# Later places for evictions, norms, shares and loads in a period of sixteen steps, and a later bias addition

## The reference

```python
xn = (x - mean) / sqrt(var + 1e-5)
q, k, v = split_heads(xn @ Wq.T), split_heads(xn @ Wk.T), split_heads(xn @ Wv.T)
diff_sq = max(|q|^2 + |k|^2 - 2 q.k, 0)
cosh_arg = 1 + 2 * diff_sq / max((1 - |q|^2) * (1 - |k|^2), 1e-6)
attn = softmax(-arccosh(cosh_arg))
out = (attn @ v) @ Wo.T
w = int4_rounded(kernel)
ffn = xn @ w + bias + (xn @ a) @ b
```

## Time and profile before

| | us |
|---|---|
| median of 3 runs | 2607.86 (2605.85 to 2612.83) |
| profiled execution, time | 2615.11 |
| its span | 2613.4 |
| TensorE busy | 2318.2 (89%) |
| ScalarE busy | 2159.3 (83%) |
| VectorE busy | 2086.7 (80%) |
| GpSimd busy | 252.1 (10%) |

### The profile page before, as it was taken

The page is one execution under the profiler, slowest core; times in us unless marked ns, Lnnn a source line. Parts: engine busy times, 40 slices in busy tenths (PEclk is TensorE's granted clock), DMA queues, the critical chain, the costliest instruction groups (busy, mean ns, idle before and its releaser), DMA issues. The chain is left out here.

```text
span 2613.4 us, 44986 instructions
## 1 busy us (share of the span) xinstructions
PE 2318.2 (89%) x17416; PEld 810.0 (31%) x17416; DVE 2086.7 (80%) x2780; ACT 2159.3 (83%) x2022; POOL 252.1 (10%) x75
## 2 busy tenths in 40 slices
PE   4889989999999999999999999999999999977774
PEld 1433333333333333333333333333333333321111
DVE  7778878888887888887888888888888887866663
ACT  2258898889888888988898888888889888999990
POOL 1011011101101110110111011011101101000000
PEclk8999999999999999999999999999999999999997
DMA  3542332444244343534524433443435344243314
GB/s 124 147 133 70 78 101 81 122 120 126 88 120 133 93 110 112 144 93 118 133 82 121 127 113 106 122 133 93 110 113 135 100 113 125 81 129 84 84 39 118
DMA packets 357001, 285.82 MB, mean 109 GB/s; under 512 B 81296, under 2 KB 296464, under 8 KB 356784
## 3 DMA queue, kind: packets, MB, share of 16 engines
q1 hardware_dynamic: 356784, 282.91, 39.3%
HBM read 160.30 MB, written 121.63 MB: 108 GB/s over the span
## 5 line engine op out<-in xcount | busy, mean ns | idle before, releaser
L416 ACT ACTIVATE root<-pU 128x1024 f32<-128x1024 f32 x1024 | 1016.0, 1027 | 31.5 <-PE pU L189 31.1
L420 ACT ACTIVATE root<-root 128x2048 f32<-128x2048 f32 x512 | 981.0, 1916 | 58.1 <-DVE root L653 56.2
L189 PE MATMUL pU<-QS,KS 100*128 100x512 f16 x2048 | 623.0, 387 | 175.9 <-ACT root L416 172.7
L653 DVE TENSOR_SCALAR root<-root 128x2048 f32<-128x2048 f32 x512 | 627.7, 1226 | 82.1 <-ACT root L416 78.8
L658 DVE TENSOR_TENSOR root<-root 128x2048 f32<-128x2048 f32 x256 | 584.5, 2283 | 14.9 <-ACT root L420 13.7
L199 PE MATMUL pO<-root,VX 128*32 128x512 f32 x4096 | 556.0, 613 | 2.3 <-ACT root L420 2.3
L767 POOL TENSOR_TENSOR xt<-xt,bias_b 128x512 f32<-128x512 f32 x64 | 243.3, 3803 | 1908.3 <-DVE xn L552 1901.6
L189 PEld LDWEIGHTS pU<-QS,KS 100*128 100x128 f16 x2048 | 139.6, 98 | 727.8 <-ACT root L416 387.3
L213 PE MATMUL pZ<-root,ones 128*32 128x512 f32 x2048 | 276.7, 611 | 1.0 <-DVE root L658 1.0
L565 DVE TENSOR_REDUCE nrm<-sqr 128x16 f32<-128x512 f32 x128 | 87.5, 683 | 144.7 <-ACT sqr L445 144.7
L257 PE MATMUL pM<-Wvh,xT 128*128 128x512 f16 x512 | 181.5, 399 | 2.6 <-ACT qk L441 2.6
(11 more groups left out here) (106 smaller groups left out, 2253.2 us busy)
## 6 DMA issues: line engine op xcount, KB each, us to landing
v_d<-v_o SPq DMA_DIRECT2D x64, 264.0 KB, 2.1
k_d<-kx SPq DMA_DIRECT2D x64, 264.0 KB, 2.1
KT<-k_d SPq DMA_DIRECT2D x64, 264.0 KB
VX<-v_d SPq DMA_DIRECT2D x64, 264.0 KB
xt<-in_x SPq DMA_DIRECT2D x32, 512.0 KB, 4.6
res_d<-f_o SPq DMA_DIRECT2D x64, 256.0 KB, 2.1
QS<-qh_d SPq DMA_DIRECT2D x128, 128.0 KB
KS<-kh_d SPq DMA_DIRECT2D x128, 128.0 KB
```

The costliest lines, as they stand in the source:

```text
L189: mm = pe.matmul(pU[:, col:col + HALF], KS[i][:, h, j * P:(j + 1) * P], QS[i][:, h, half * HALF:(half + 1) * HALF], start=True, stop=True)
L416: act.activation(root[:, q % RING, cols], pU[:, cols], ACT.Square).then_inc(squared, 1)
L420: act.activation(root[:, q % RING, :], root[:, q % RING, :], ACT.Sqrt).then_inc(rooted, 1)
L653: v.tensor_scalar(root[:, q % RING, :], root[:, q % RING, :], CS * CS, CS * CS, ALU.max, ALU.subtract).then_inc(clamped, 1)
```

## The change

Nothing is computed otherwise. In each engine's `behind` and in ScalarE's loop the step at which a piece stands is another:

- TensorE: f's projection of even periods at steps 12 and 13 (was 13 and 14).
- ScalarE: pO's copy after the square of step 5 (was before that of step 4), pZ's after step 8 (was before step 6), v's eviction at 8 (was 7), the variance's root at step 0 of the next even period (was 14 of the odd one).
- VectorE: norms at 4 and 6 (were 3 and 5), `normalise` at 7 (6), `aug_rows` at 9 (8), `inverse` at 2 (0), `divide` at 1 (4), `take_f` at 14 in even periods and at 0 of the next period for odd ones (15).
- GpSimd: the bias addition of a tile also waits until q of that tile is transposed, two periods later than before.
- SP: stores of attention, k and extra rows one step later, the first half of a stack's load behind KV's copies (step 13, was 9), the other half in step 3 of the odd period, f's store and x's load with the later `take_f`.

```diff
--- before.py
+++ after.py
@@ -329,12 +329,10 @@
                         elif n + 1 < NT:
                             pe.wait_ge(x_split, n + 2)
                         transpose_feat(n, 0, 0 if even else 1)
-                    if even and k == 13:
+                    if k == 12:
                         pe.wait_ge(feat_split[0], n + 1)
-                    if not even and k == 12:
-                        pe.wait_ge(feat_split[0], n + 1)
-                    if even and k in (13, 14):
-                        project(n, "f", 0, 6 * k - 78, 6 * k - 72)
+                    if even and k in (12, 13):
+                        project(n, "f", 0, 6 * k - 72, 6 * k - 66)
                     elif not even and k in (12, 13, 14):
                         project(n, "f", 1, 4 * k - 48, 4 * k - 44)
                     if even and k == 14:
@@ -457,10 +455,10 @@
                         take_qk(n, 0, 0)
                     elif k == 4:
                         take_qk(n, 1, 1)
-                    elif k == 7:
+                    elif k == 8:
                         take_v(n, 1)
-                if k == 14 and p % 2 and n + 3 < NT:
-                    deviation((n + 3) // 2)
+                if k == 0 and p % 2 == 0 and p and n + 2 < NT:
+                    deviation((n + 2) // 2)
 
             deviation(0)
             deviation(1)
@@ -476,16 +474,16 @@
                 take_v(n, 1 - n % 2)
                 if n % 2:
                     deviation((n + 3) // 2)
-            for s in range(16 * PERIODS + 8):
+            for s in range(16 * PERIODS + 9):
                 p, k = s // 16, s % 16
-                if k == 4 and p:
-                    take_v_sums(p - 1)
-                if k == 6 and p:
-                    take_one_sums(p - 1)
                 if s < 2 * QUADS:
                     square(s)
+                if k == 5 and p:
+                    take_v_sums(p - 1)
                 if s % 2 and 0 <= (s - 3) // 2 < QUADS:
                     sinh((s - 3) // 2)
+                if k == 8 and p:
+                    take_one_sums(p - 1)
                 if p < PERIODS:
                     behind(p, k)
 
@@ -660,25 +658,26 @@
             def behind(p, k):
                 n, o, even = p + LEAD, p - LEAD, p % 2 == 0
                 if n < NT:
-                    if k == 0 and even and n + 2 < NT:
+                    if k == 2 and even and n + 2 < NT:
                         inverse((n + 2) // 2)
-                    if k == 3:
+                    if k == 4:
                         norm(n, 0)
                     if k == 5 and n + 1 < NT:
                         split_x(n + 1, 0)
-                    if k == 5:
+                    if k == 6:
                         norm(n, 1)
                         factors(n)
-                    if k == 6:
                         scale_qk(n)
-                        if n + 2 < NT:
-                            normalise(n + 2)
-                    if k == 8:
+                    if k == 7 and n + 2 < NT:
+                        normalise(n + 2)
+                    if k == 9:
                         aug_rows(n)
                 if k == 0 and p % 2 and n - 1 < NT:
                     split_feat(n - 1, 1, 1)
+                if k == 0 and even and p and n - 1 < NT:
+                    take_f(n - 1, 1)
                 if o >= 0:
-                    if even and k == 4:
+                    if even and k == 1:
                         divide(o)
                     if k == (9 if even else 10):
                         take_o(o, 0)
@@ -694,8 +693,8 @@
                 if n < NT:
                     if k == 14 and not even and n + 3 < NT:
                         moments((n + 3) // 2)
-                    if k == 15:
-                        take_f(n, 0 if even else 1)
+                    if k == 14 and even:
+                        take_f(n, 0)
 
             dve.up(v.memset(ones[:, :], V_SCALE))
             dve.up(v.memset(flag[:, :], 0.0))
@@ -764,6 +763,8 @@
             def add_bias(n):
                 t = xt[n // 2 % 3][:, n % 2, :]
                 g.wait_ge(xn_done, n + 1)
+                if n >= LEAD:
+                    g.wait_ge(featT_made[0], n + 1)
                 g.tensor_tensor(t, t, bias_b[:, :], ALU.add).then_inc(xb_done, 1)
 
             def everywhere(dst, col, after):
@@ -906,21 +907,13 @@
                     load_res(o)
                 if k == 8 and n < NT:
                     store_v(n)
-                if k == 8 and p:
+                if k == 9 and p:
                     store_att(p - 1)
                 if k == 9 and last_of_block:
                     load_z((o + 1) // TPB, p)
-                if k == 9 and n < NT:
+                if k == 10 and n < NT:
                     store_k(n)
                     store_aug(n)
-                if k == 9 and even and 2 <= p and p // 2 + 1 < PERIODS // 2:
-
-                    sy.wait_ge(summed_up, p * JC)
-                    if (p // 2 + 1) % KC == 0:
-                        all_stored(n)
-                    load_stack(p // 2 + 1, 0)
-                    if (p // 2 + 1) % KC:
-                        load_stack(p // 2 + 1, 1)
                 if k == (10 if even else 11) and o >= 0:
                     store_out(o)
                 if k == 12 and not even and o >= 0 and not last_of_block and o + 1 < NT:
@@ -932,11 +925,21 @@
                     store_feat(n)
                 if k == 12 and even:
                     pass_kv(p)
-                if k == 15 and n < NT:
+                if k == 13 and even and 2 <= p and p // 2 + 1 < PERIODS // 2:
+
+                    sy.wait_ge(summed_up, p * JC)
+                    if (p // 2 + 1) % KC == 0:
+                        all_stored(n)
+                    load_stack(p // 2 + 1, 0)
+                if k == 3 and not even and 3 <= p and p // 2 + 1 < PERIODS // 2 and (p // 2 + 1) % KC:
+                    load_stack(p // 2 + 1, 1)
+                if k == 15 and even and n < NT:
                     store_f(n)
-                    if not even and n + 5 < NT:
-                        sy.wait_ge(var_done, (n + 3) // 2)
-                        load_x((n + 5) // 2)
+                if k == 1 and even and p and n - 1 < NT:
+                    store_f(n - 1)
+                    if n + 4 < NT:
+                        sy.wait_ge(var_done, (n + 2) // 2)
+                        load_x((n + 4) // 2)
 
             load_x(0)
             sy.dma_start(idn[:, :], io["ident"]).then_inc(small_loaded, 16)
```

## The result

The changed kernel takes 2471.64 us (2470.7 to 2475.46, 4 runs) against 2608.57 us: a ratio of 0.9476, interval 0.946 to 0.9493. That is 137 us less, where 118 were forecast (2490, range 2450 to 2560).

What follows compares the result with a forecast made beforehand. TensorE and ScalarE in lockstep bound the kernel; 108 us from the main stretch, 14 from the first, 3 from the last, less 8 for divisors, gave 117 off the profiled 2615.1; less 7.3 for the median: 2490 us, range 2450 to 2560.

Steps and rivals of the forecast that it cites:

- What bounds the kernel: Main stretch: TensorE and ScalarE run in lockstep, TensorE the busier; its waits, 88.6 us for squares and 34.6 for KV, are winnable.
- Copies of pO and pZ: ScalarE: pO's copy, behind square 5, finds its sum ready; its 1.05 us idleness and TensorE's 0.63 us at step 5 go.
- KV: SP's queue: KV's copies go ahead of the stack loads, about 5.5 us earlier, so TensorE's 34.6 us of waits go.
- F's projection: TensorE steps 12 and 13: no work added; VectorE's step 15 no longer waits, so its next clamp is not late.
- the written-out pair: Starts of squares and TensorE's steps listed through two periods: 73.7 to 74.7 us before, 35.6 + 34.7 = 70.3 after.
- Bias: GpSimd's addition runs beside `split_feat`; VectorE gets 1.1 us a period back, off the path, so counted as nothing.
- Divisors: Every fourth period V's later copy delays z: wait from 0.53 to about 1.7 us, 14 blocks, 8 us lost.
- Division from step 4 to 1, and the norms one step later: VectorE: 3.1 us leave steps 4 and 5, where clamps were queued; step 8's clamp ends about 1 us before needed.
- What would show it: List of expected profile signs, such as a pair near 72 us, and of signs that would prove the prediction wrong.
- the correction of 1.6 us a pair: Added to the 70.3 us pair, giving 71.9, because the same method was 1 to 2 us too good for before.
- The rival with nearly all waits gone: Nearly all TensorE waits go, plus the matmul pipeline's emptying at each wait: 2608 - 155 = 2453 us; chance 0.2.
- The one with a new wait at `sum_v`: TensorE, level with square 4, waits 1.0 us for pO's copy at step 5, 56 periods: 2546 us; chance 0.15.

Runs made afterwards that it cites:

- the kernel with two tiles: The changed kernel with a tile of squares each for q and k, so k's square no longer waits for q's norm: 2437.98 us, ratio 0.9342.
- two experiments: Two edits of the changed kernel: a squares' tile each for q and k, 2437.98 us; the division at step 4 again, 2434.65 us.

## Why the prediction was right, and where it was off

**What bounds the kernel** was right: two engines in lockstep, TensorE the busier. With the extra waits removed the time falls nearly to TensorE's own sum: a pair of 70.2 us in the kernel with two tiles, against 69.3 worked out.

**Copies of pO and pZ**: the mechanism was right, shown by undoing it (28 us) and doing it alone (47 us). The two copies were always moved together, so how the gain is shared between them is not shown. "The copy finds it ready" holds: ScalarE's wait for pO is gone.

**KV**: right in kind, too small. I put down the 34.6 us of waits. Alone it gave 50, undone it cost 59. The rest is in the main the lower clock behind ten of the waits, which was not in the sum at all.

**F's projection** gave 21 us; I had no separate price for it, only its place in the written-out pair. **Bias**: counted at nothing, measured within 4 us of it. **Divisors**: 8 us lost by the forecast, from a wait of 1.7 us per block. The wait is 2.0 us, and moving V's store out of the way gave 11 us in the kernel with two tiles.

**The step that failed** is "Division from step 4 to 1, and the norms one step later". I followed the clamps through VectorE's queue and found play for each, but overlooked the one tile of squares between ScalarE and VectorE. The square of k at step 4 waits for q's norm, which stood at step 3 and now stands at step 4, behind the division. For `sum_v` of step 5 in even periods I wrote "no wait" in the part on the copies and 0.46 us in the sum; it is 1.79, and two experiments price it at 34 and 37 us. In "What would show it" a wait there of 1 us a period was named as the sign of a wrong forecast; it came at 1.8 us in every second period, 0.9 a period.

**Why the total came out near all the same.** In the main stretch the forecast was 108 us, or about 101 with the divisors' loss, which falls mostly there, and 108.6 was measured. That is luck: two errors cancel. The missed wait cost 34 us there. Against it, the correction of 1.6 us a pair (38 us in 24 pairs), which I took over from the kernel before because its written-out pair had been too good, was not due. The slow slices were about 0.9 us a pair of that shortfall before, and they are gone; the rest of it is not explained. With the wait removed the pair is 70.2 us, and written out without the correction it was 70.3.

The first stretch gave 22 for 14 us, and the slow slices of it, 8.5 us in the kernel before and none now, were not in my sum; the last gave 13 for 3. In the last, ScalarE's idle time fell from 16 to 5 us: the copy of pZ had waited there 6.8 us and the squares 7.6, and I had counted hardly any of it. TensorE's clock cost 11.9 us there before and 1.7 after, which the sum did not have either; how much of it reached the time is not shown. In all the sum gave 117 us for these executions, and 144 were measured.

The rival with nearly all waits gone (2453) is near what the kernel is with the second tile (2438). Its own terms, 123, 20 and 24 us, add up to 167 and not to the 155 that it takes off: 2441. The one with a new wait at `sum_v` had the right place and a wrong cause. I argued that TensorE reaches the sum too early; in fact the copy was late, because the square of k ahead of it waited for the norm.

## What to carry to other kernels

When work is moved later in a hand-written order, go through every buffer that the moved piece reads: whoever overwrites it next may now wait too, and between engines in lockstep such a wait can be passed on in full, as 1.58 us of ScalarE's were here. Price a wait of TensorE with what the clock does behind it, and compare the granted clock of both stretches before a shortfall is put down to the method. Read an experiment by stretch before its cause is named: the two parts that were worth more together were so at the ends of the kernel alone. And undo parts of a successful change one by one: here one of them cost 37 us, and it hid that another was worth 28.

## What the runs showed of the hardware

TensorE, busy for 93% of the main stretch, fell to 1.2 GHz behind single waits. In the kernel before ten of its 15 waits for KV of 1.7 us and more had such a stretch behind them, of some 3 to 7 us each, and five of seven waits of 1.92 us in the first periods. In the changed kernel 23 waits of 1.79 us at the sum of V had none in 1720 us. In the run with the copies of pO alone at their new places only 2 of 18 waits for KV between 460 and 2180 us had one, among them waits of 3.00 and 2.57 us without one. So the length of one wait does not decide it. Nor does the further wait of 0.64 us a step later, which stands in the rows above: there the clock fell before that wait was over, and the waits for KV that ended at 507.67 and 1579.94 us had it too, and no slow stretch. What decides it stays open.

A bias addition of GpSimd held up one operation of VectorE in each period, large or small: the 128x16 one in the kernel before (1.30 us; 0.16 to 0.17 in the changed one), the clamp in the run with the early addition (2.30 us for 1.22). It was itself held up behind the pair sum and the clamp in the one (4.4 us) and behind the pair sum alone in the other (3.25 us), and what decides that is not shown. Beside `split_feat`, in the changed kernel, it took 1.28 us.
